# A short GpSimd write behind each move of rows, in place of waits for TensorE's progress

## The reference

```python
x = x + 0.5 * ffn(layernorm(x))      # layer 1
x = x + attn(layernorm(x))           # layer 2
x = x + 0.5 * ffn(layernorm(x))      # layer 3

def ffn(x):                          # shared expert plus 2 of 8 routed experts
    shared = (silu(x @ sg.T) * (x @ su.T)) @ sd.T
    p = sigmoid(x @ router.T + bias)
    scores, idx = top_k(p, 2); scores /= scores.sum(-1)
    g = silu(x @ gate_w[e]); u = x @ up_w[e]
    return shared + sum over the two chosen e of scores[e] * (g * u) @ down_w[e]
```

## Time and profile before

| | |
|---|---|
| median of three runs | 479.21 us |
| span of the profiled execution | 501.9 us |
| granted TensorE clock, mean | 0.995 |
| instructions in the span | 9741 |
| DMA, mean over the span | 107 GB/s |

### The profile page before, as it was taken

One profiled execution on the slowest core, in us unless ns is written; L12 is line 12 of the kernel. 1 busy time (PEld: TensorE's weight loads), 2 busy tenths in 40 slices (PEclk: granted clock), 3 DMA queues, 4 the chain that ended last, 5 costly groups with the idle time before them and its releaser, 6 DMA issues.

```text
span 501.9 us, 9741 instructions
## 1 busy us (share of the span) xinstructions
PE 462.0 (92%) x2975; PEld 382.8 (76%) x2975; DVE 346.8 (69%) x1064; ACT 271.0 (54%) x612; POOL 282.3 (56%) x290
## 2 busy tenths in 40 slices
PE   8979899989899999899989998999998998999896
PEld 4868678877788787688767877877776777888776
DVE  4999993333568865868889898899876532454355
ACT  5936135555476555476546664655464555565421
POOL 4148556665567245566636655686654555666562
PEclk9999999999999999999989999999999999999999
DMA  8981233253421334321132322114342253543323
GB/s 237 370 283 39 68 107 116 80 167 113 111 73 64 101 80 116 92 68 57 54 102 56 91 75 74 43 39 123 88 128 84 78 163 105 150 113 104 86 73 106
DMA packets 74353, 53.68 MB, mean 107 GB/s; under 512 B 9664, under 2 KB 68928, under 8 KB 74304
## 3 DMA queue, kind: packets, MB, share of 16 engines
q1 hardware_dynamic: 66112, 36.26, 24.4%
q0 software_dynamic: 8192, 16.79, 11.0%
HBM read 26.87 MB, written 26.15 MB: 106 GB/s over the span
## 4 chain that ended last, share of the span: by engine, by line
PE 50%; DVE 26%; issue 10%; ACT 6%; another core or an unknown queue 5%; DMA 2%; POOL 0%; SPq 0%; DVEq 0%; ACTq 0%; POOLq 0%
PE pool L888 12%; PE pool L877 6%; PE gu L843 5%; PE gu L845 5%; PE gu L844 5%; DVE X L1242 3%; PE gu L804 2%; DVE hs L1219 2%; PE pool L826 2%; DVE hs L1223 2%; PE gu L802 2%; DVE raw L1421 2%; PE gu L803 2%; DVE stats L1253 2%
## 5 line engine op out<-in xcount | busy, mean ns | idle before, releaser
L1176 POOL DMA_INDIRECT yg<-y_sorted,places x128 | 124.2, 970 | 94.3 <-PE gu L845 42.0
L1156 POOL DMA_INDIRECT x_sorted<-xn,places x128 | 129.7, 1013 | 83.3 <-PE gu L845 30.8
L1219 DVE TENSOR_TENSOR hs<-gs,gu 128x512 f32<-128x512 f32 x92 | 60.7, 663 | 89.4 <-ACT gs L1033 64.7
L1033 ACT ACTIVATE gs<-gu 128x512 f32<-128x512 f32 x124 | 72.1, 583 | 70.8 <-PE gu L804 24.8
L888 PE MATMUL pool<-w,hT 128*128 x708 | 99.3, 283 | 11.6 <-ACT hT L1039 9.7
L888 PEld LDWEIGHTS pool<-w,hT 128*128 128x128 f32 x708 | 87.6, 191 | 26.4 <-issue 23.0
L843 PE MATMUL gu<-w,xbt_hi 128*128 x177 | 81.8, 462 | 1.8 <-DVE xbt_lo L1205 1.5
L1039 ACT ACTIVATE hT<-pool 128x512 f32<-128x512 f32 x92 | 53.3, 580 | 36.2 <-PE pool L877 24.8
L845 PE MATMUL gu<-w,xbt_hi 128*128 x177 | 70.0, 396 | 0.0
L844 PE MATMUL gu<-w,xbt_lo 128*128 x177 | 69.9, 395 | 0.0
L1014 ACT ACTIVATE ys<-pool 128x256 f32<-128x256 f32 x92 | 34.5, 376 | 62.6 <-PE pool L888 34.2
(11 more groups left out here) (132 smaller groups left out, 786.8 us busy)
## 6 DMA issues: line engine op xcount, KB each, us to landing
xb<-x_sorted SPq DMA_DIRECT2D x85, 128.0 KB
y_sorted<-ys SPq DMA_DIRECT2D x85, 128.0 KB
x_sorted<-yg SPq DMA_DIRECT2D x6, 512.0 KB, 6.3
X<-x_dram SPq DMA_DIRECT2D x8, 256.0 KB, 4.8
x_sorted<-xn,places POOLq DMA_INDIRECT x128
yg<-y_sorted,places POOLq DMA_INDIRECT x128
out_dram<-X SPq DMA_DIRECT2D x8, 256.0 KB
raw<-gate_w_dram SPq DMA_DIRECT2D x4, 256.0 KB, 4.8
```

The lines of the kernel that those rows point to most:

```text
L1033: nc.scalar.activation(dst, src, ACT.Silu).then_inc(silu_done, 1)
L1156: nc.gpsimd.indirect_dma_start(x_sorted[g], bass.IndirectOffsetOnAxis(places[g][:, k, t:t + 1], 0), xn[:, b, t % T], None).then_inc(scatte ...
L1176: nc.gpsimd.indirect_dma_start(yg[slot][:, k, t], None, y_sorted[g], bass.IndirectOffsetOnAxis(places[g][:, k, at:at + 1], 0)).then_inc(ga ...
L1219: v.tensor_tensor(hs[n % HB][:].rearrange("p (j i) -> p j i", j=2)[:, 0:k], gs[n % GB][:].rearrange("p (j i) -> p j i", j=2)[:, 0:k], bank ...
```

## The change

`pace` goes: moves no longer wait for `half_ready` and `gu_ready`. Behind each move GpSimd writes zeros to 384 one-byte elements in each of 128 partitions, a region that nobody reads any more (the triangle in `squares_sb`, after ScalarE has copied it). Each such write waits for the one before it, by a semaphore of its own. At its start GpSimd waits once for ScalarE's copy. The order of all other instructions on all engines, the plan and its numbers are the same.

```diff
--- before.py
+++ after.py
@@ -1,4 +1,5 @@
 from contextlib import ExitStack
+from itertools import count as counter
 
 import numpy as np
 import concourse.bass as bass
@@ -12,6 +13,7 @@
 F32R = mybir.dt.float32r
 BF16 = mybir.dt.bfloat16
 I32 = mybir.dt.int32
+U8 = mybir.dt.uint8
 
 B, S, D = 8, 512, 128
 T = S // P
@@ -37,6 +39,7 @@
 HOP_PE, ADDRESS = 20, 11
 LOADED, COLD = 4, 340
 WARM = 20
+PARTED = 384
 LETTERS = "".join(chr(c) for c in range(35, 126) if c not in (39, 92))
 URGENCY = (
     "WLFWSb^ukX}PPPnPCcJNT;RELRIJR8=6@K?didXL<:VH0&UF>CSFKJaSYsKdP]JRNN5L3reTK/]YP[UOTFBVLWXSmQM{YMeWcIMPVu]/PKNPLU"
@@ -572,6 +575,7 @@
         ve, rstd = sb("ve", [P, 4, B, T]), sb("rstd", [P, 4, B, T])
         shifts = sb("shifts", [P, 4, B, T])
         minus_half = sb("minus_half", [P, T])
+        spare = squares_sb[:, 1].bitcast(U8)[:, 0:PARTED]
 
         groups = range(NG)
         wsel = [sb(f"wsel{g}", [P, 2, tiles(g)]) for g in groups]
@@ -665,7 +669,7 @@
         rden_done, widened, rbc_ready, rbc_done = (sem(n) for n in ("rden_done", "widened", "rbc_ready", "rbc_done"))
         conv0_done, conv_link, num_ready, att_done = sem("conv0_done"), sem("conv_link"), sem("num_ready"), sem("att_done")
         o_sum_done, oT_done, proj_ready = sem("o_sum_done"), sem("oT_done"), sem("proj_ready")
-        stored = sem("stored")
+        stored, parted = sem("stored"), sem("parted")
 
         def wait(eng, s, value):
             if value > 0:
@@ -1137,11 +1141,12 @@
                 once.wait_ge(ln_link[l], (b + 1) * LN_LINKS)
                 nc.gpsimd.tensor_tensor(rstd[:, l, b], ve[:, l, b], minus_half[:], ALU.pow).then_inc(rstd_done[l], 1)
 
-            def pace(*key):
-
-                half_through, through = plan.through(key)
-                wait(once, half_ready, half_through)
-                wait(once, gu_ready, through)
+            parts = counter()
+
+            def part_moves():
+
+                wait(once, parted, next(parts))
+                nc.gpsimd.memset(spare, 0).then_inc(parted, 1)
 
             def scatter(g, n):
                 t, k = n // 2, n % 2
@@ -1152,10 +1157,10 @@
                     once.wait_ge(blanked[g], 16 * -(-ROOM // BLANK))
                 if n == 0 and g >= ROOMS:
                     once.wait_ge(xbt_ready, first_pair[g - ROOMS] + pairs(g - ROOMS))
-                pace("scatter", g, n)
                 nc.gpsimd.indirect_dma_start(
                     x_sorted[g], bass.IndirectOffsetOnAxis(places[g][:, k, t:t + 1], 0),
                     xn[:, b, t % T], None).then_inc(scattered[g], 16)
+                part_moves()
 
             def gather(l, b, n):
                 g = group_of(l, b)
@@ -1172,10 +1177,10 @@
                         for i in range(ROOMS):
                             once.wait_ge(blanked[i], 16 * -(-ROOM // BLANK))
                 at = GROUPS[g].index((l, b)) * T + t
-                pace("gather", l, b, n)
                 nc.gpsimd.indirect_dma_start(
                     yg[slot][:, k, t], None, y_sorted[g],
                     bass.IndirectOffsetOnAxis(places[g][:, k, at:at + 1], 0)).then_inc(gathered[b], 16)
+                part_moves()
 
             nc.gpsimd.memset(ones_bf[:], 1.0).then_inc(ones_set, 1)
             nc.gpsimd.memset(minus_half[:], -0.5).then_inc(half_set, 1)
@@ -1184,6 +1189,7 @@
             nc.gpsimd.memset(vT[1][:], 0.0)
             nc.gpsimd.memset(v_tok[:], 1.0).then_inc(pads_set, 1)
             once.wait_ge(half_set, 1)
+            once.wait_ge(earlier_done, 1)
 
             run("POOL", {"root": root, "scatter": scatter, "gather": gather})
```

## The result

The changed kernel takes 491.8 us (median of four executions, 491.47 to 492.52), the kernel before 479.33 us (477.92 to 480.57). The ratio is 1.0254, 95% interval 1.0229 to 1.0279: 12.2 us slower, where 478.7 was forecast. The case that came about is the rival called "GpSimd becomes the bound", but not by its reason: the write costs what was forecast.

What follows compares the result with a forecast made beforehand. TensorE, busy 92% of the span, was taken as the bound, with hardly anyone waiting for GpSimd. A gain of 1.2 us and a loss of 0.7 gave -0.5 us: 478.7 us, range 476.8 to 481.6 (8 in 10: 475.0 to 485.5).

Steps and rivals of the forecast that it cites:

- GpSimd becomes the bound: Rival, 20%: the write costs more than its elements; at 1.70 us from move to move the time is 483.2 us.
- The cost of the write: On GpSimd, from memsets at the start: a record of 0.42 us, giving 1.60 us from move to move.
- the wait at GpSimd's start: GpSimd's new wait for ScalarE's copy: nothing, with 0.96 us to spare before the first root.
- The last stretch: The last 48 gathers on GpSimd: at 1.60 us each against 1.599, the last gather comes 0.05 us later.
- the alternative that the text did not take: Stretches run 4.5% faster when timed while GpSimd's instructions keep their length: last gather 3.3 us late.
- What the new spacing does to each stretch: 1.60 us against old averages of 1.636 (first stretch) and 1.599 (last): GpSimd neither set free nor made the bound.
- a term that had been priced: 18 of 24 roots queue behind a write, 0.36 to 0.42 us each; VectorE's shift and ScalarE's normalisation wait behind them.
- What reaches the end: The sum over the span: -1.2 us at the sixth group's load, +0.7 at VectorE's add, together -0.5 us.
- The forecast gain of 1.2 us: The sixth group's last scatter begins earlier, so TensorE's 1.16 us wait for its first load goes: -1.2 us.
- The loss at the adds: VectorE's add at 443.74 waits for a gather now 0.7 us later, with TensorE queued behind: up to +0.7 us.
- The last adds: At the end, the last add follows TensorE's last products; a gather 0.05 us later changes nothing.
- Moves run ahead: Rival, 22%: a cheaper, packed memset, 1.37 us from move to move; waits of 1.8 and 1.3 us go: 476.3 us.

Runs made afterwards that it cites:

- the second execution: The kernel before, unchanged, profiled once more: 481.15 us in one execution, with a span of 479.3 us.
- words_96: The changed kernel with the same 384 bytes written as 96 four-byte elements: 480.27 us, ratio 1.0004 to the kernel before.
- write_192: The changed kernel with half the write, 192 one-byte elements in place of 384: 479.56 us, ratio 0.9992 to the kernel before.
- no_wait_no_write: The changed kernel without the writes, the waits for TensorE gone too: 479.94 us, ratio 0.9986 to the kernel before.
- write_512: The changed kernel with a longer write, 512 one-byte elements in place of 384: 514.44 us, ratio 1.0708 to the kernel before.

## Why the prediction was wrong

**Right steps.** The cost of the write (0.42 forecast, 0.435 measured), its spacing (1.60 forecast, 1.57 measured between neighbouring moves without a long record), that GpSimd's zeros are not packed, and that the wait at GpSimd's start costs nothing. The last stretch was missed by little: forecast 0.05 us longer, measured 1.35 against the second execution, between that and the 3.3 us of the alternative that the text did not take.

**The step that failed** is "What the new spacing does to each stretch". It compared 1.60 with the average spacing of the old moves, 1.599 and 1.636, and concluded that GpSimd is neither set free nor made the bound. The runs showed GpSimd as the bound in every stretch where its moves, the writes and their gaps no longer fit: the fourth group's scatters became 2.3 us longer, the fifth's 3.7, the last 48 gathers 1.35. Three things were wrong in the step.

First, it used two stretches, and most of the loss arose between them. The view of the trace that lays the span out in windows (length, then busy time of each engine and its instructions, granted clock, DMA share, GB/s) would have shown it in the very execution that the prediction had. The scatters of the fourth group and of the fifth, each from the first's start to the last's:

```profile
221.34:248.38 27.04, 25.74 (x173) 22.35 (x172) 23.20 (x59) 18.81 (x43) 18.88 (x18) 1.00 0.18 60
303.48:342.08 38.60, 36.17 (x228) 29.25 (x226) 34.66 (x88) 21.92 (x49) 26.73 (x26) 1.00 0.16 55
```

In the fifth group's line GpSimd is busy for 26.73 us, 23 scatters and two roots. Adding 23 writes of 0.435 (10.0) and the gaps of 0.17 behind 21 of them and 0.14 around each of two roots (3.9) makes 40.6 us, 2.0 more than the 38.60 there are. The fourth group's line, with 17 moves (two gathers among them) and a root, makes 18.88 + 7.4 + 2.9 = 29.2, or 2.1 too much for 27.04. The first stretch gives 67.50 + 28.3 + 11.0 = 106.8 of 109.26 and the last 45.52 + 20.4 + 8.0 = 73.9 of 75.15: both fit, and only these two stand in the prediction.

Second, the average held more than moves. In the fifth group's stretch it is (38.60 - 2 x 0.97) / 23 = 1.594, just under 1.60 and so harmless by the prediction's reading. But 1.60 was made with a record of 0.95, while the mean record of a scatter was 1.013, and the average contains such long records. They come on top of 1.60; the sum over busy time has them in.

Third, the execution was 4.7% too long, and most of its stretches with it, while GpSimd's instructions had their usual length (mean records of 1013 and 1024 ns for a scatter, 970 and 980 for a gather). The room in these stretches was too large by as much: 2.2 us in the fifth group's, 2.6 in the last; in the fourth group's there was no such excess. In the execution of 479.3 us the same windows are these, the scatters of the fourth and fifth groups and the last 48 gathers:

```profile
213.74:241.07 27.33, 26.19 (x180) 23.17 (x179) 23.19 (x58) 19.48 (x43) 19.26 (x19) 1.00 0.18 59
292.57:329.01 36.44, 36.01 (x234) 30.12 (x233) 34.94 (x89) 22.11 (x49) 27.40 (x26) 1.00 0.18 60
397.52:470.09 72.57, 71.38 (x453) 61.21 (x452) 36.36 (x87) 37.46 (x82) 45.28 (x48) 1.00 0.41 110
```

The sums are 19.26 + 7.4 + 2.9 = 29.6 for 27.33, or 2.2 too much, 27.40 + 10.0 + 3.9 = 41.3 for 36.44, or 4.9, and 45.28 + 20.4 + 8.0 = 73.7 for 72.57, or 1.1. In the changed kernel:

```profile
216.82:246.42 29.60, 27.75 (x192) 24.70 (x191) 25.53 (x69) 19.53 (x43) 26.73 (x35) 1.00 0.18 57
298.16:338.31 40.15, 37.82 (x238) 31.20 (x237) 36.55 (x91) 22.27 (x49) 36.23 (x48) 1.00 0.15 52
406.89:480.81 73.92, 72.68 (x455) 61.83 (x455) 36.16 (x88) 37.97 (x82) 65.50 (x94) 1.00 0.40 108
```

40.15 is 36.23 busy and 3.9 of gaps: nothing else fits in. The stretches became 2.3, 3.7 and 1.35 us longer. The text had seen the third point ("if the stretches run 4.5% faster in a timed execution while GpSimd's instructions keep their length") and refused it, since the waits follow TensorE. That reason doesn't hold here: in the fifth group's stretch and in the last the excess room was there in the long execution alone.

Besides, a term that had been priced is missing from the sum: 0.36 to 0.42 us for each root behind a write, for which VectorE's shift and ScalarE's normalisation wait. VectorE's wait for roots grew by 6.6 us.

**What reaches the end.** The forecast gain of 1.2 us, TensorE's wait for the sixth group's load, came to 0.3 (a wait of 1.67 us before, 1.36 after), and three other groups now wait as well, since their scatters became later and not earlier:

```profile
169.73 0.44 PE L830 MATMUL pool<-squares_sb,xb 128*128 128x128 f32 x2 [0.39 <-DMA xb<-x_sorted]
251.06 0.91 PE L830 MATMUL pool<-squares_sb,xb 128*128 128x128 f32 x4 [1.65 <-DMA xb<-x_sorted]
343.30 0.44 PE L830 MATMUL pool<-squares_sb,xb 128*128 128x128 f32 x2 [0.29 <-DMA xb<-x_sorted]
397.64 0.44 PE L830 MATMUL pool<-squares_sb,xb 128*128 128x128 f32 x2 [1.36 <-DMA xb<-x_sorted]
```

These are TensorE's turns in the changed kernel, each with its wait for sorted rows in brackets. The loss at the adds was of the right kind (5.6 us of waiting for gathers in place of 2.4). The last adds, which were to hang on TensorE alone, now wait 0.56 us for the last gather:

```profile
483.37 1.14 DVE L1248 SCALAR_TENSOR_TENSOR X<-yg,wsel,X 128x128 f32<-128x128 f32 x4 [0.56 <-DMA yg<-y_sorted,places]
```

What was left out is the way through the groups. GpSimd works its list in order: a late scatter makes the gathers and roots behind it late, then the norms, products and loads that wait for those, and then the next group's scatters. The chain of the changed kernel's page goes along GpSimd's list at 255 to 282 us (gathers and roots), at 298 to 342 (the fifth group's scatters, a gather and roots) and from 394 to the last gather, with VectorE's and TensorE's work between. So the lateness of one group stays in all that follows (8.6 us at the fifth group's first pair, 9.4 at the last stretch's first gather). TensorE's waits for sorted rows make up 2.0 of the 10.4 us; how the rest divides among the other waits is open.

**The rivals.** "Moves run ahead" needed a cheaper write; `words_96`, `write_192` and `no_wait_no_write` show that even with a cheaper write, or none, nothing is won, so its 3 us were not there to win. "GpSimd becomes the bound" was right in its mechanism. Its rule of 0.47 us at the end for each 0.01 us of spacing counted the 47 gaps of the last stretch alone and is too small: from 384 to 512 elements the spacing grows by 0.107 us and the time by 22.6, 2.1 us for each 0.01. Its threshold was too late: 1.65 was given, from the last stretch; the runs put it between 1.42 (no loss) and 1.57 (12.2 us).

## What to carry to other kernels

Whether an engine has room for added work is read stretch by stretch: its busy time there, plus the added instructions, plus their gaps, against the length of the stretch, the most crowded one first; the average spacing of instructions that were held by waits does not show it. An engine off the critical path may lie idle for 40% of the span, as GpSimd did, and still cost time when work of 23% of the span is added, since it needs the rest to make up for holds and long records where its work is dense. And when a profiled execution is some per cent longer than the timed ones, profile the program again before reading a stretch's room: the excess need not lie evenly in the stretches.

## What the runs showed of the hardware

**A write on GpSimd goes by elements, not by bytes or partitions.** 96 elements of four bytes took 196 ns, 192 of one byte 276, 384 of one byte 435, 512 of one byte 542; with 384 of one byte, one partition in place of 128 took 408, only 6% less. That is about 0.83 ns for each element ((542 - 276) / 320) and some 0.12 us fixed.

**A short instruction of VectorE can get longer beside GpSimd.** The prediction read L1263's mean of 181 ns as showing no blocking. In the second execution of before its records are 169 to 328 ns; the same instruction after the change:

```profile
L1269 DVE TENSOR_SCALAR ve<-mv x24: 169/172/755, 4.9 to 351.2; 128x4 f32<-128x4 f32 x24
```

(min, median and max in ns.) Of the 24 records, 11 are longer than 0.2 us, and ten of these end within 0.03 us of the end of an instruction on GpSimd, as here of a write and of a gather:

```profile
149.55 0.44 POOL L1149 MEMSET squares_sb<- 128x384 uint8 x1
149.75 0.27 DVE L1269 TENSOR_SCALAR ve<-mv 128x4 f32<-128x4 f32 x1
...
339.88 0.99 POOL L1180 DMA_INDIRECT yg<-y_sorted,places  x1 [0.16 <-issue]
340.11 0.76 DVE L1269 TENSOR_SCALAR ve<-mv 128x4 f32<-128x4 f32 x1
340.19 0.69 DVE L1229 TENSOR_TENSOR hs<-gs,gu 128x512 f32<-128x512 f32 x1
```

The ends are 149.99 and 150.02, 340.87 and 340.87. But three records keep 0.17 us inside a gather on GpSimd, as here:

```profile
261.28 0.96 POOL L1180 DMA_INDIRECT yg<-y_sorted,places  x1 [0.16 <-issue]
261.42 0.17 DVE L1269 TENSOR_SCALAR ve<-mv 128x4 f32<-128x4 f32 x1
261.50 0.74 DVE L1427 SCALAR_TENSOR_TENSOR raw<-vT,taps,raw 128x512 f32<-128x512 f32 x1
```

The next record of VectorE starts 0.08 us behind the start of L1269 in both cases, whether that is long (340.19) or short (261.50), so a long record does not show by itself that VectorE's later work is held up. The Trainium skill, page "SBUF — State Buffer", section "Who interferes with whom", states that of an instruction of VectorE in a two-port mode and an instruction of GpSimd the one that starts first holds the ports they share for its whole length, and the other waits. The trace agrees for the ten long records and not for the three short ones; in which mode they ran no run shows. The estimate from it was 1.1 us on this line; its 24 records went from 4.3 to 6.3 us, 2.0 more, and VectorE's busy time from 345.2 to 348.5. In `write_512` they again took 6.3 us, while the time rose by another 22.6: the loss does not go with this line. What the longer records cost by themselves wasn't measured.
